# Denominators of a linear attention: one fp32 product, or two fp32r products of halves that GpSimd splits off, two product groups later

## What is computed

```python
q = jax.nn.elu(q) + 1.0
k = jax.nn.elu(k) + 1.0
k_cum = jnp.cumsum(k, axis=1)
kv = jnp.cumsum(k[..., None, :] * v[..., :, None], axis=1)
numerator = jnp.einsum('bthj,bthij->bthi', q, kv)
denominator = jnp.einsum('bthj,bthj->bth', q, k_cum)
out = numerator / (denominator[..., None] + 1e-06)
out = out * gate
```

## Time and profile before

| | |
|---|---|
| median of 3 runs (lowest to highest) | 863.05 us (862.45 to 865.03) |
| profiled execution | 857.38 us |
| its span, first to last instruction | 855.6 us |
| mean granted TensorE clock | 0.976 |
| TensorE busy | 811.2 us, 95% |
| VectorE busy | 640.4 us, 75% |
| ScalarE busy | 560.4 us, 66% |
| GpSimd busy | 244.8 us, 29% |
| steps r = 1 to 7 | about 146 to 397 us |

### The profile page before, as it was taken

One profiled execution on the slowest core, in us unless ns is written; L12 is line 12 of the kernel. 1 busy time (PEld: TensorE's weight loads), 2 busy tenths in 40 slices (PEclk: granted clock), 3 DMA queues, 4 the chain that ended last, 5 costly groups with the idle time before them and its releaser, 6 DMA issues.

```text
span 855.6 us, 24099 instructions
## 1 busy us (share of the span) xinstructions
PE 811.2 (95%) x9254; PEld 703.5 (82%) x9254; DVE 640.4 (75%) x1032; ACT 560.4 (66%) x878; POOL 244.8 (29%) x149
## 2 busy tenths in 40 slices
PE   6799989999999999999988999999999999999994
PEld 4466568899999899897967789888888898889883
DVE  3544443747657476664685999999999999999992
ACT  2443547646536465463233998898999989998981
POOL 2344300000000000000001255564445554554541
PEclk9999999999999999999696999999999999999997
DMA  9999920000000000004861255445545554555452
GB/s 351 404 414 416 414 107 2 2 16 3 27 16 14 28 2 27 2 27 157 348 250 56 82 150 142 124 139 155 133 124 138 153 138 123 142 146 140 123 139 45
DMA packets 31770, 115.91 MB, mean 135 GB/s; under 512 B 4465, under 2 KB 11570, under 8 KB 26578
## 3 DMA queue, kind: packets, MB, share of 16 engines
q1 hardware_dynamic: 22834, 100.17, 32.5%
q0 software_dynamic: 8864, 14.69, 8.0%
HBM read 105.27 MB, written 9.57 MB: 134 GB/s over the span
## 4 chain that ended last, share of the span: by engine, by line
PE 84%; DMA 6%; DVE 5%; issue 2%; ACT 2%; SPq 0%; POOLq 0%; DVEq 0%; ACTq 0%
PE ps L471 22%; PE ps L473 21%; PE ps L472 21%; DMA ctx_t<-in_ctxT 5%; PE ps L836 4%; PE ps L661 3%; PE ps L640 2%; PE ps L649 1%; PE ps L529 1%; PE ps L716 1%; PE ps L799 1%; PE ps L570 1%; PE ps L787 1%; DMA bor<-in_bo 1%; PE ps L722 1%
## 5 line engine op out<-in xcount | busy, mean ns | idle before, releaser
L1491 DVE TENSOR_TENSOR w_lo<-w,w_hi 128x1024 fp32r<-128x1024 f32 x156 | 186.4, 1216 | 1.4 <-issue 1.4
L1056 ACT ACTIVATE w_hi<-w 128x1024 fp32r x156 | 161.4, 1061 | 2.4 <-DVE tile_e L1542 2.4
L457 POOL DMA_INDIRECT out_x<-y_sb,slot_row x39 | 121.6, 3118 | 120.0 <-ACT y_sb L1088 120.0
L471 PE MATMUL ps<-w_hi,xh 128*128 128x512 f32 x312 | 125.7, 403 | 1.3 <-DVE xl L1582 1.3
L473 PE MATMUL ps<-w_hi,xl 128*128 128x512 f32 x312 | 122.0, 391 | 0.0
L472 PE MATMUL ps<-w_lo,xh 128*128 128x512 f32 x312 | 121.5, 390 | 0.0
L471 PE MATMUL ps<-xT_hi,wa_hi 128*128 128x256 f32 x384 | 111.9, 291 | 0.4 <-DVE kT L1271 0.4
L472 PE MATMUL ps<-xT_lo,wa_hi 128*128 128x256 f32 x384 | 107.5, 280 | 1.0 <-issue 1.0
L473 PE MATMUL ps<-xT_hi,wa_lo 128*128 128x256 f32 x384 | 107.4, 280 | 0.0
L1067 ACT ACTIVATE w_hi<-w_sb 128x1024 fp32r<-128x1024 f32 x78 | 82.6, 1062 | 30.6 <-DMA w_sb<-in_w 19.0
L445 POOL DMA_INDIRECT xs_sb<-xn_d,slot_row x39 | 68.6, 1759 | 101.1 <-PE ps L799 80.1
(11 more groups left out here) (208 smaller groups left out, 1747.1 us busy)
## 6 DMA issues: line engine op xcount, KB each, us to landing
w_sb<-in_w SPq DMA_DIRECT2D x78, 512.0 KB, 4.4
ctx_t<-in_ctxT SPq DMA_DIRECT2D x16, 1028.0 KB, 10.2
ctx_n<-in_ctxN SPq DMA_DIRECT2D x16, 1024.0 KB
w<-in_w SPq DMA_DIRECT2D x8, 2048.0 KB, 14.2
stage<-in_w_a SPq DMA_DIRECT2D x16, 256.0 KB, 9.2
x_all<-in_x SPq DMA_DIRECT2D x4, 512.0 KB, 8.7
out_x<-x_all POOLq DMA_DIRECT2D x8, 256.0 KB, 3.2
xn_d<-xn_first POOLq DMA_DIRECT2D x6, 256.0 KB, 3.0
```

Of the source, the lines that this page charges most:

```text
L457: pool.indirect_dma_start(out, bass.IndirectOffsetOnAxis(slot_row[:, t:t + 1], 0), y_sb[:, :], None, compute_op=ALU.add).then_inc(f_st, 16)
L471: pe.matmul(dst, l_hi, r_hi, start=first, stop=False)
L1056: act.activation(w_hi[:, c, :].rearrange("p (c n) -> p c n", c=DC), w13[:, bass.ds(e, 1), c % 2, :, c // 2 * 512:(c // 2 + 1) * 512].rearr ...
L1491: dve.tensor_tensor(w_lo[:, c, :].rearrange("p (c n) -> p c n", c=DC), w13[:, bass.ds(e, 1), c % 2, :, c // 2 * 512:(c // 2 + 1) * 512].re ...
```

## The change

The denominators of the steps 0 to 6 are made another way; those of step 7 stay as they are (`a_dens` in the drain).
- GpSimd rounds each masked half of `att` to fp32r (`att_hi`) and subtracts (`att_lo`), two instructions for each parity h, and rounds the summing matrix once (`twos_r`). TensorE makes two fp32r products for each tile from them.
- The denominators move from behind the second group of queries and keys to behind the fourth, on TensorE and on ScalarE. VectorE's reciprocals and the first normalization move back among the elus, the fourth reciprocal behind the eighth elu.
- The new buffers lie where the weights of expert 1 will be, so that expert's load moves behind the one of expert 0.
- GpSimd's DMA issues are written in another order, so that the split of a step stands ahead of the issues whose data come later.

```diff
+    SPLIT_AT = W13_AT + EXP_BYTES
+    att_hi = nc.alloc_sbuf_tensor_at("att_hi", [P, 2, FC, 2, T], F32R, offset=SPLIT_AT)
...
-        load_expert(1)
         sp.wait_ge(a_v, 4 * NT // 2)
         sp.wait_ge(a_gt, 4 * NT // 2)
         for e in range(E // 2, E):
             load_expert(e)
         sp.wait_ge(g_tr, XN_T // 2)
         sp.wait_ge(g_keep, 16 * XN_T // 2)
         load_expert(0)
+        load_expert(1)
...
+        def att_split(r):
+            wait(pool, a_den, 2 * r)
+            for h in range(2):
+                pool.wait_ge(a_att, 2 * r + h + 1)
+                pool.tensor_copy(att_hi[:, :, :, h, :], att[:, :, :, h, :]).then_inc(a_sh, 1)
+                pool.wait_ge(a_sh, 2 * r + h + 1)
+                pool.tensor_tensor(att_lo[:, :, :, h, :], att[:, :, :, h, :], att_hi[:, :, :, h, :].bitcast(F32),
+                                   ALU.subtract).then_inc(a_sl, 1)
...
+        def a_dens_split(r):
+            pe.wait_ge(a_two, 1)
+            wait(pe, a_sl, 2 * r + 2)
+            for s in range(2):
+                rows = lambda t: t[:, s, :, :, :].rearrange("p c h t -> p (c h t)")
+                pe.matmul(ps[:, 4 + s, :], twos_r[:, :], rows(att_hi), start=True, stop=False)
+                pe.matmul(ps[:, 4 + s, :], twos_r[:, :], rows(att_lo), start=False, stop=True).then_inc(a_den, 1)
...
-                a_qks(r, range(0, 2))
-                a_dens(r - 1)
-            a_qks(r, range(2 if before else 6, 8))
+                a_qks(r, range(0, 4))
+                a_dens_split(r - 1)
+            a_qks(r, range(4 if before else 6, 8))
```

More of the change, by code:

```diff
@@ L198, in build @@
     assert at["late"] <= TOP_ADDR - 2 * DC * 4 * HF * 4
+    SPLIT_AT = W13_AT + EXP_BYTES
+    att_hi = nc.alloc_sbuf_tensor_at("att_hi", [P, 2, FC, 2, T], F32R, offset=SPLIT_AT)
+    att_lo = nc.alloc_sbuf_tensor_at("att_lo", [P, 2, FC, 2, T], F32R, offset=SPLIT_AT + 4 * 2 * FC * 2 * T)
+    twos_r = nc.alloc_sbuf_tensor_at("twos_r", [P, P], F32R, offset=SPLIT_AT + 8 * 2 * FC * 2 * T)
     in_slot = nc.alloc_sbuf_tensor_at("in_slot", [P, NT * TOP, P], F32R, offset=at["low"])
@@ L319, in build @@
     o_init = sem("o_init")
+    a_sh, a_sl, a_two = (sem("a_" + n) for n in ("att_hi", "att_lo", "twos"))
     (f_xs, f_xtr, f_xh, f_xl, f_up, f_dn, f_uhi, f_ulo, f_dhi, f_dlo, f_silu, f_h, f_t, f_hh, f_hl, f_y,
@@ L431, in _, with keep_x @@
                                    hi_all[:, bass.ds(t * SW, SW)].bitcast(F32), ALU.subtract).then_inc(s_split_lo, 1)
-        for r in range(NT // 2):
+        NR = NT // 2
+        def keep_x(r):
             rows = slice(2 * r * P, (2 * r + 2) * P)
@@ L436, in _, with keep_xn @@
             pool.dma_start(out[rows, :].rearrange("(t p) d -> p t d", p=P), x_all[:, 2 * r:2 * r + 2, :]).then_inc(o_init, 16)
+        def keep_xn(r):
+            rows = slice(2 * r * P, (2 * r + 2) * P)
             pool.wait_ge(g_ln, 2 * r + 2)
@@ L439, in _ @@
                 g_keep if 2 * r < XN_T else g_keep2, 16)
+        def att_split(r):
[6 more added lines that the diff above has]
+                                   ALU.subtract).then_inc(a_sl, 1)
+        pool.tensor_copy(twos_r[:, :], con[:, C_TWOS:C_TWOS + P]).then_inc(a_two, 1)
+        for r in range(NR - 1):
+            att_split(r)
+            if r < NR - 2:
+                if r > 0:
+                    keep_xn(r - 1)
+                keep_x(r)
+        for r in range(NR - 2, NR):
+            keep_xn(r - 1)
+            keep_x(r)
+        keep_xn(NR - 1)
         def gather(t):
@@ L995, in astep @@
             if before:
-                elu_parts(r, range(0, 2))
+                elu_parts(r, range(0, 4))
                 den_ev(r - 1)
-            elu_parts(r, range(2 if before else 6, 8))
+            elu_parts(r, range(4 if before else 6, 8))
             gates(r, u, range(4) if r < NR - 1 else range(3))
@@ L1347, in astep @@
                 masks(r - 1)
-            if r > 0:
-                elu(r, 0)
-                elu(r, 1)
+            if before:
+                for n in range(3):
+                    elu(r, n)
                 recip(r - 1, 0)
[L1352 to L1355, removed]
                 elu(r, 3)
                 elu(r, 4)
-                recip(r - 1, 2)
+                recip(r - 1, 1)
+                norm_att(r - 1, 0)
                 elu(r, 5)
             elu(r, 6)
-            recip(r - 1, 3)
+            if before:
+                recip(r - 1, 2)
             elu(r, 7)
             if before:
+                recip(r - 1, 3)
                 norm_att(r - 1, 1)
```

## The result

| | before | changed |
|---|---|---|
| median, lowest to highest | 862.98 us (862.45 to 865.03) | 857.28 us (854.2 to 858.15) |
| ratio, 95% interval | | 0.9922 (0.9902 to 0.9942) |
| profiled execution | 857.38 us | 857.08 us |
| TensorE busy | 811.2 us | 808.6 us |

The change gains 5.7 us, and I had forecast 1.2 with at most 4.5 inside my range: wrong. The two profiled executions are no measure of it: that of before was 5.6 us under its median, that of after 0.2 us under its own. I had noted that difference in the prediction and carried it along as a constant.

A forecast was written before the change was run, and what follows sets the result against it. TensorE, busy 95%, was taken as the bound, VectorE only 0.25 us behind. Step gains of 0.1 to 0.2 us made 1.25, taking the profiled 857.38 to 856.1; with 5.7 to the median, 861.8 us, range 858.5 to 866.0.

The forecast's parts named there:

- The products: Denominators: four fp32r products at 0.23 us replace two fp32 taking 1.72, saving TensorE 0.79 us in each of seven steps.
- The split: GpSimd's rounds (0.62 us) and subtractions (1.27) end at about 5.05 us after the masks start, hidden by 0.3 us.
- rival B: Steps: TensorE waits for GpSimd's slower rounding and subtracting; 866.5 us at 1.5 times the duration, 880 at twice; chance 0.11.
- The order around them: Attention steps: VectorE's eighth elu hardly moves, so TensorE waits about 0.6 of its 0.79 us; gain 0.2 per step.
- Rival A: Seven steps: TensorE keeps the whole gain, 5.5 us, giving 857.5; chance 0.11 together with half of it.
- The load: Drain: expert 1's 2 MB load moves there, needing 5.4 us of queue time, covered by 8 us; costs nothing.
- the sum over the steps: Steps r = 1 to 7: 0.2 us in five, 0.15 in r = 5, 0.1 in r = 1; together 1.25 us.
- the closing of the sum: Whole kernel: profiled 857.38 us goes to 856.1; the median's 5.7 us excess is applied to it, giving 861.8.
- signs of being wrong: Early first reciprocal, eighth elu off by over 0.3 us, TensorE waiting for GpSimd, or drain over 2 us longer or shorter.
- Rival C: Drain: TensorE's 2.13 us stall at 400.10 and half clock shift; stall more 865, less 859; chances 0.07 slower, 0.06 faster.

The follow-up runs named there:

- load_late: Kernel before with only the load of expert 1's weights moved behind that of expert 0; 863.00 us, ratio 0.9983 (0.9953 to 1.0013).
- The pairs: Kernels without and with the change, at equal added TensorE waits or equal instruction places; differences -2.1, -3.7, -1.8 (16, 32, 128 waits), -1.6 and -4.4 us.
- before_again: Kernel before, unchanged, run again for a second trace and more times; 864.06 us, ratio 0.9984 (0.9955 to 1.0013).
- before_waits: Kernel before with one more wait for an already set semaphore on TensorE in each of steps 0 to 6; 861.69 us, ratio 0.9986.
- after_hold: Changed kernel with the loads of experts 4 to 7 held back until the last step's scores are through; 857.48 us, ratio 0.9918.
- the padded kernels: Kernel before or changed kernel with 16 to 192 added TensorE waits near 17 us; kernel before 861.34 us at 16, 878.79 at 192.

## Why the prediction was wrong, by its own steps

- **The products, right.** 0.79 us saved a step; 0.77 fewer busy. Four products 0.23 apart, as forecast.
- **The split, right.** 0.61 and 1.27 to 1.30 us for runs of 32 numbers, the speed of the contiguous ones; rival B fell at once. Only r = 1, whose masks come late, waits for it, 1.43 us at 152.75, and takes 35.57 us where it took 35.60: that wait fell into an old one, as I had said.
- **The order around them, right.** First reciprocal M+8.21 for M+8.20, eighth elu M+16.26 for M+16.24 or so, TensorE's wait 0.46 to 0.56 us for some 0.6, 0.14 to 0.21 us gained in a whole step for the 0.15 of the sum. The numerators of r = 6 start at M+18.58, where I had M+18.4 to 18.5, so not all of the 0.2 has been gained by then. Rival A, that TensorE keeps its 0.8 us, gives nearly the measured time, 857.5, and is false: a number that fits is no proof of a mechanism.
- **The load, right.** load_late measured nothing.
- **The step that failed first is the sum over the steps**, "together 1.25 us". It counted what the change does to one undisturbed step and put at nothing the idle stretches that stand in the others. The steps fell by 3.7 us against the profiled execution that the sum was made from, and by 4.9 against the second. In r = 6 alone it is 2.3 and 2.1 us where I had 0.2, and the 0.64 and 1.00 us that went there stood in the trace that I had read.
- **The second is the closing of the sum**: "the median of 863.05 lies 5.7 above it, and I apply the difference to it". The profiled execution was one of the quickest of its kernel, by a drain of 69.0 us. The changed kernel's own took 857.08, with a drain of 71.8: 2.8 us longer, which is one of the signs of being wrong that I had named (a drain over 2 us longer or shorter). The difference to the median is no constant of the kernel, since it holds the drain's clock and stretches of one execution.
- **Rival C pointed at one of the stretches, with the wrong mechanism.** I had the stall of 2.13 us at 400.10 before me, said that nothing names it, tied it to the loads, and gave it "a stall less 859" (861.8 less 2.13 is 859.7) at a chance of 0.06. I had looked at none of the others (0.68 us ahead of 292.91, 0.64 and 1.00 us in r = 6), and of the queue that carries instructions only at its share, 0.5%. Together the stretches were worth 2.9 us between two executions. They belonged in the sum as a term of unknown sign, and the range, whose low end was 858.5, had no room for them.

What is shown: the change's own mechanism, 0.2 us a step; that the idle stretches stand at fixed instructions, 256 apart, and end with a fetch; that seven instructions that do nothing, put into the kernel before, take them off r = 6, and six taken out of the changed one bring them back. What is only likely: that the 5.7 us are some 1 to 3 us of the change itself and the rest the places. The pairs (-1.6 to -4.4 by the medians) agree with that, but their differences are as uncertain as they are large, and the forecast 1.25 us is neither confirmed nor refuted by them as the change's own part. What stays open: after the hole in the last scores the granted clock is at the lower level for a while in some traces, and not in others with a hole of the same length. In before_again and in the changed kernel, the windows that follow the hole:

```profile
402.92:404.92 2.00, 2.00 (x10) 2.00 (x11) 1.89 (x5) 0.00 (x0) 0.00 (x0) 0.50 0.99 426
```
```profile
397.12:399.12 2.00, 2.00 (x18) 2.00 (x19) 1.89 (x5) 0.00 (x0) 0.00 (x0) 1.00 1.02 434
```

At 0.50, the 1.2 GHz level, TensorE begins 10 products where it begins 18 at 1.00. The first profile of before, with a hole of 2.13 us, has no such stretch there; before_waits, with 1.81, has one; after_hold, with 1.81, has none. The clock is a large part of the spread of the drain, 69.0 to 73.4 us: TensorE is busy for 61.7 us of it at a mean of 0.80, for 67.8 at 0.72, with the same 584 products. What decides the clock I can't say.

## What to carry to other kernels

A gap marked "issue" that recurs at the same instruction in every execution is not noise: look at the instruction queue's packets, and count instructions, not microseconds, between such gaps. Where a kernel has runs of products shorter than a fetch covers, any edit of TensorE's program, even a satisfied wait, shifts all that stands behind it and can move the time by some us in either direction; judge an edit at two or three shifts before believing a gain of that size. And take a second execution of the kernel before, when the profiled one is off the median by more than the effect that is forecast.

## What the runs showed of the hardware

- TensorE runs dry at its instruction supply, at places that lie a multiple of 256 instructions apart, and only in or just behind runs of small products: up to 2.4 us of idle time (3.7 in the padded kernels), ended 2.2 to 2.9 us after a 16 KB packet of the instruction queue starts (3.2 in one case of 121), with or without other DMA traffic.
- Instructions that wait for a semaphore that has long been set: 16 or 32 in a row, behind products, lengthened TensorE's idle time there by 0.2 us in all; from 64 to 192 each added 0.10 to 0.11 us, nearly the pace of a product of 0.113.
- GpSimd's subtraction of 128x512 takes 1.27 to 1.30 us on runs of 32 numbers as on contiguous rows.
